# Transposing the next batch's normalised rows on VectorE instead of TensorE

## The reference

```
x = x + LayerNorm(x + relu(x @ W1 + b1) @ W2 + b2) * gamma + beta      # layer 0: x1
x = x + x @ W.T + b                                                    # layer 1: x2
x = x + gated sum of two experts and three shared nets,                # layer 2: x3
        each relu(x @ wi) @ wo with 1024 hidden features
x = x + masked attention pooling of x / count                          # layer 3: out
```

## Time and profile before

| | |
|---|---|
| median of 3 runs | 502.25 us (502.12 to 503.63) |
| the profiled execution's own time | 501.93 us |
| its span in the profile | 500.1 us |
| TensorE busy | 493.7 us, 99% |
| VectorE busy | 349.2 us, 70% |
| ScalarE busy | 260.9 us, 52% |
| GpSimd busy | 235.8 us, 47% |
| TensorE's granted clock | full (2.4 GHz) in all slices |

### The profile page before, as it was taken

How to read it: one execution, slowest core, us unless ns; L and a number is a source line. 1 busy time by engine, 2 the same in 40 slices (tenths; PEclk the granted TensorE clock), 3 DMA queues, 4 the chain that set the end, 5 groups by cost and what they waited for, 6 DMA issues and landing times.

```text
span 500.1 us, 7007 instructions
## 1 busy us (share of the span) xinstructions
PE 493.7 (99%) x2327; PEld 408.6 (82%) x2327; DVE 349.2 (70%) x703; ACT 260.9 (52%) x507; POOL 235.8 (47%) x201
## 2 busy tenths in 40 slices
PE   8999999999999999999999999999999999999996
PEld 5788888888888888888888888888888888888984
DVE  5687226884687799785578689788468779644477
ACT  4655554443457574535346666444345757445234
POOL 1684455445354446444644437444535444745022
PEclk9999999999999999999999999999999999999999
DMA  5865454222265442422227453422222342330002
GB/s 156 185 184 148 111 154 142 86 85 85 86 128 141 116 112 86 127 83 89 80 90 185 105 178 107 127 84 85 85 85 85 102 109 84 102 132 22 0 1 84
DMA packets 77657, 52.97 MB, mean 106 GB/s; under 512 B 40758, under 2 KB 67382, under 8 KB 77622
## 3 DMA queue, kind: packets, MB, share of 16 engines
q1 hardware_dynamic: 75734, 50.44, 35.6%
q10 hardware_dynamic: 1888, 2.10, 1.4%
HBM read 48.33 MB, written 2.10 MB: 101 GB/s over the span
## 4 chain that ended last, share of the span: by engine, by line
PE 98%; DVE 1%; ACT 1%; issue 0%; POOL 0%; DVEq 0%
PE ps_hid L838 14%; PE ps_hid L839 14%; PE ps_hid L843 14%; PE ps_net L900 14%; PE ps_net L895 14%; PE ps_net L896 14%; PE ps_net L867 2%; PE ps_side L537 1%; PE ps_side L541 1%; PE ps_side L536 1%; PE ps_side L547 1%; PE ps_side L550 1%; PE ps_hid L687 1%; PE ps_side L730 1%; PE ps_net L666 1%; PE ps_hid L638 0%
## 5 line engine op out<-in xcount | busy, mean ns | idle before, releaser
L1915 POOL TENSOR_TENSOR wi_lo<-raw_wi,wi_hi 128x512 fp32r<-128x512 f32 x77 | 101.6, 1319 | 207.0 <-ACT wo_hi L1088 109.8
L1109 ACT ACTIVATE hid_hi<-ps_hid 128x512 fp32r<-128x512 f32 x160 | 95.5, 598 | 194.9 <-PE ps_hid L843 193.1
L1823 DVE SCALAR_TENSOR_TENSOR hid_lo<-ps_hid,hid_hi 128x512 fp32r<-128x512 f32 x160 | 109.8, 688 | 114.0 <-ACT hid_hi L1109 112.8
L838 PE MATMUL ps_hid<-x2T_hi,wi_lo 128*128 128x512 f32 (+1 forms) x332 | 125.8, 381 | 0.0
L839 PE MATMUL ps_hid<-x2T_hi,wi_hi 128*128 128x512 f32 (+1 forms) x332 | 125.3, 379 | 0.0
L895 PE MATMUL ps_net<-hid_hi,wo_hi 128*128 128x512 f32 x304 | 118.9, 391 | 0.0
L896 PE MATMUL ps_net<-hid_hi,wo_lo 128*128 128x512 f32 x304 | 118.4, 390 | 0.0
L1916 POOL TENSOR_TENSOR wo_lo<-raw_wo,wo_hi 128x512 fp32r<-128x512 f32 x77 | 104.1, 1352 | 0.0
L843 PE MATMUL ps_hid<-x2T_lo,wi_hi 128*128 128x512 f32 (+1 forms) x332 | 98.9, 379 | 0.0
L900 PE MATMUL ps_net<-hid_lo,wo_hi 128*128 128x512 f32 x304 | 94.0, 390 | 0.0
L839 PEld LDWEIGHTS ps_hid<-x2T_hi,wi_hi 128*128 128x128 f32 x332 | 62.5, 188 | 11.8
(11 more groups left out here) (330 smaller groups left out, 502.7 us busy)
## 6 DMA issues: line engine op xcount, KB each, us to landing
raw_wi<-in_L_cond_share_wi_dram SPq DMA_DIRECT2D x23, 512.0 KB, 3.8
raw_wo<-in_L_cond_share_wo_dram SPq DMA_DIRECT2D x23, 512.0 KB, 4.8
raw_wi<-in_L_cond_expert_wi_dram SPq DMA_DIRECT2D x16, 512.0 KB, 3.8
raw_wo<-in_L_cond_expert_wo_dram SPq DMA_DIRECT2D x16, 512.0 KB, 4.8
next_x2T<-in_x_dram SPq DMA_DIRECT2D x24, 64.0 KB, 4.3
x_rows<-in_x_dram SPq DMA_DIRECT2D x3, 512.0 KB, 4.0
x_rows<-netT SPq DMA_DIRECT2D x48, 32.0 KB, 2.0
out_dram<-out_rows SPq DMA_DIRECT2D x5, 256.0 KB, 5.6
```

The costliest lines, as they stand in the source:

```text
L838: mm(dst, wi_lo[:, w, k, c], x2T_hi[:, k, rows], start=(k == 0), stop=False)
L1109: fn(hid_hi[:, ring(b, q)], ps_hid[:, ring(b, q)], ACT.Relu).then_inc(hid_hi_ready, 1)
L1823: v.scalar_tensor_tensor(out=hid_lo[:, ring(b, q)], in0=ps_hid[:, ring(b, q)], scalar=0.0, in1=f32(hid_hi[:, ring(b, q)]), op0=ALU.max, op ...
L1915: g.tensor_tensor(wi_lo[:, w], raw_wi[:, half % 2, :, c], f32(wi_hi[:, w]), ALU.subtract)
```

## The change

TensorE's transposes of the normalised rows are taken out, with their two semaphore steps. VectorE does them instead. It can transpose 32x32 blocks; to bring block (a, c) of the rows to its place, each instruction takes the 32 partitions of group `a` and writes the 32 partitions of group `c`: 16 instructions for 4 x 4 pairs of groups, each for all 8 (k, r) pairs, 256 elements to a partition. Eight stand in slot 30 and eight in slot 31. They write `next_x2T`, free since slot 21. The scale by gamma and the addition then read this buffer instead of PSUM, both halves in slot 32 behind `xb`, which moves there too. To make room, stage A from `w2` to `norm` runs one slot earlier. `x1_hi`, `x1_lo`, `y` and `base` keep their slots. `adapt` on VectorE gets a wait for its own `subj_w_lo`.

```diff
-    A_SLOT = dict(w1=20, blocks=20, xT=22, w2=25, subj_blocks=25, hid=26, subj_w=27, adapt=28, stats=29, xb=31, norm=30, normT=32, x1_hi=33, x1_lo=35, y=36, base=37)
+    A_SLOT = dict(w1=20, blocks=20, xT=22, w2=24, subj_blocks=24, hid=25, subj_w=26, adapt=27, stats=28, xb=32, norm=29, turn=30, x1=32, x1_hi=33, x1_lo=35, y=36, base=37)
...
+        normT = next_x2T
...
-            def normalised(slot, i):
-                if 0 <= slot - A_SLOT["normT"] < KD:
-                    k = slot - A_SLOT["normT"]
-                    pe.wait_ge(a_dve.sem, a_dve.at(i, "norm"))
-                    for r in range(R):
-                        last = nc.tensor.transpose(ps_side[:, k, r * P:(r + 1) * P], norm[:, r, k * P:(k + 1) * P], ident[:])
-                    last.then_inc(a_pe.sem, 1)
...
+                if slot == A_SLOT["x1"]:
+                    here("turn1")
+                    for k in range(KD):
+                        here(f"xb{k}")
+                        v.scalar_tensor_tensor(out=x1T[:, k], in0=normT[:, k], scalar=gamma[:, k:k + 1], in1=xbT[:, k],
+                                               op0=ALU.mult, op1=ALU.add).then_inc(a_dve.sem, 1)
...
+                if 0 <= slot - A_SLOT["turn"] < 2:
+                    h = slot - A_SLOT["turn"]
+                    here("norm")
+                    for a in (2 * h, 2 * h + 1):
+                        last = turn_rows(a)
+                    last.then_inc(a_dve.sem, 1)
...
+            def turn_rows(a):
+                for c in range(P // BK):
+                    rows = norm[a * BK:(a + 1) * BK].rearrange("p r (k d) -> p k r d", d=P)[:, :, :, c * BK:(c + 1) * BK]
+                    cols = normT[c * BK:(c + 1) * BK].rearrange("p k (r s) -> p k r s", s=P)[:, :, :, a * BK:(a + 1) * BK]
+                    last = v.transpose(cols, rows)
+                return last
```

More of the change, by code:

```diff
@@ L276, in cond_resid_program @@
         evac_dve = Steps(sem("evac_dve"), "g0 g1 g2 g3")
-        a_pe = Steps(sem("a_pe"), "hid adapt0 adapt1 normT0 normT1 y0 y1", 1)
+        a_pe = Steps(sem("a_pe"), "hid adapt0 adapt1 y0 y1", 1)
         a_act = Steps(sem("a_act"), "xhi0 xhi1 hid_below hid_up subj_w_hi x1hi0 x1hi1", 1)
         a_dve = Steps(sem("a_dve"), "w1_hi xT0 xT1 xlo0 xlo1 w2_hi w2_up b2_hi b2_lo subj_wT hid_sum hid_hi hid_lo subj_w_lo sum0 sum1 stats sums mean var_eps "
-                                    "norm xb0 xb1 x1T0 x1T1 x1lo0 x1lo1 x2T0 x2T1", 1)
+                                    "norm turn0 turn1 xb0 xb1 x1T0 x1T1 x1lo0 x1lo1 x2T0 x2T1", 1)
         a_pool = Steps(sem("a_pool"), "w1_lo w2_lo rstd", 1)
@@ L913, in batch @@
                         second_product(b, s, first, last)
-                    if not last:
-                        normalised(q, b + 1)
                     if not first:
@@ L1251, in stage_a @@
                     dve.wait_ge(x_in, 16 * i)
+                    here("subj_w_lo")
                     for t in range(2):
```

## The result

The changed kernel takes **512.81 us** in the median of 5 runs (512.61 to 513.63) against 502.25 before: 1.0207 times as long, with a 95% interval of 1.0196 to 1.0219. Its profiled execution has a span of 510.9 us against 500.1.

What follows compares the result with a forecast made beforehand. TensorE was taken to bound the kernel. Per batch -1.00 (transposes) + 0.65 (adapter) + 3.84 (bank 0) = +3.49, +10.5 us over three batches: 512.7 us from 502.25, forecast range 510.5 to 515, wider range 504.5 to 518.

Steps and rivals of the forecast that it cites:

- What bounds the kernel: TensorE, 98% of the span: 2.72 us per slot without side work; matmuls removed are gained, waits lost, one for one.
- The removed transposes, 1.00 us a batch: Slots 32 to 34 on TensorE: taking the transposes out gains 1.00 us a batch, 3.0 in all, the whole gain.
- The adapter, +0.65 us a batch: Slot 27: TensorE waits 0.76 us instead of 0.11 for `subj_wT_lo`, +0.65 a batch; bounds 0.44 and 1.9.
- The 0.11 us that the wait was said to cost already before: Adapter's second half in the kernel before: its matmul starts about 0.11 us late, waiting for `subj_wT_lo`.
- A transpose at 0.44 us: VectorE's sixteen transposes change output group each time, so do not overlap: 0.44 us each, 7.0 a batch.
- the lower bound of 0.35: VectorE transposes: 0.35 us each if they overlap, 5.6 us a batch; 0.27 was given as the extreme.
- The order in which it goes late: Bank 0 is late next: ScalarE copies it behind `x1_hi` of half 0, and TensorE wants it in slot 34.
- The size of that wait: TensorE's wait on bank 0 in slot 34: 3.84 us a batch, released at 21.97 where 18.13 was due.
- the 3 to 4 named as its sign: Sign of being right: TensorE waits for ScalarE's `netT` three times, 3 to 4 us each.
- the fourth `norm` caught by GpSimd: VectorE's fourth `norm`, issued at 8.86, is held by GpSimd's split at 8.77: VectorE free at 10.2, otherwise 9.2.
- cheaper passage: Rival, chance 0.22: smaller bank wait through slots 29 to 33; 509.7 or 508.4 us, 505.4 with both savings.
- The clock: Within a rival of chance 0.18: TensorE falls to 1.2 GHz after the wait, 2.72 us more a batch, 520.9 us.

Runs made afterwards that it cites:

- e1_no_turn: The kernel before without TensorE's 24 transposes and nothing in their place (that part of the computation left out): 499.46 us, 0.9931 times the kernel before.
- e2_sooner_only: The kernel before with stage A from `w2` to `norm` one slot sooner, transposes still on TensorE: 504.46 us, 1.0038 times the kernel before.
- e6_both_waits: The changed kernel with `x1_hi` one slot later on ScalarE and, in slot 26, `hT_both` and `subj_wT_hi` ahead of the weight split: 500.56 us.
- e7_no_pe_wait: The changed kernel with `x1_hi` one slot later on ScalarE and without TensorE's wait for `subj_wT_lo` before the adapter's second half: 499.25 us.
- e5_same_group: The changed kernel with each of the sixteen transposes writing the partition group it reads (blocks land in wrong groups): 505.64 us.
- e3_copy_first: The changed kernel with `x1_hi` one slot later on ScalarE, so bank 0's copy no longer stands behind it: 501.37 us.
- e4_warm: The changed kernel with ten matmuls of zeros into an unused bank just ahead of TensorE's wait on bank 0: 509.92 us.

## Why the prediction was right, and where it was not

- **What bounds the kernel: right.** TensorE's slots are at 2.72 us wherever nothing makes it wait, before and after, and each term shows one for one in the table.
- **The removed transposes, 1.00 us a batch: right**, by e1_no_turn.
- **The adapter, +0.65 us a batch: right**, +0.65, +0.64 and +0.66, and e2_sooner_only shows it by itself. The mechanism was incomplete: the sum went from ScalarE to GpSimd and never asked when VectorE's queue would be free. That queue ends within 0.1 us of ScalarE's `subj_wT_hi`, so leaving it out changed nothing here, which was luck; e6_both_waits shows that it alone holds most of the wait. The 0.11 us that the wait was said to cost already before is borne out by e7_no_pe_wait, where slot 27 takes 3.71 instead of 3.84.
- **A transpose at 0.44 us: right**, measured 0.45 from start to start (8 in 3.57 and 3.59 us, 422 to 442 ns each), and e5_same_group shows the reason that was given, the change of group. With the group kept it is 0.33, a little under the lower bound of 0.35 that was given for transposes that overlap.
- **The order in which it goes late: right.** ScalarE's copy of bank 0 behind `x1_hi`, in slot 34; e3_copy_first removes nothing but that and all of it is gone.
- **The size of that wait: too large by 1.05 us a batch**, 2.79 instead of 3.84, and by the view of waits 2.5 us, under the 3 to 4 named as its sign. The step that failed is the fourth `norm` caught by GpSimd. `norm` was issued 0.3 us sooner than I had it (102.36, 7.63 into slot 28, where I had 7.93). Three things make that up. I let one small instruction of the statistics through between `wi_lo` and `wo_lo`, and two got through (0.07). The one that is held ends together with `wo_lo`, as the earlier trace rows had shown; my sum ran on as though it began there (0.16). And `wo_lo` ended 0.09 sooner than I had it. The fourth part of `norm` was then ahead of GpSimd's next instruction, which is what had to wait: the four `norm` take 1.38 us together, and `wi_lo` in slot 30 lasts 1.37 instead of 1.29. VectorE came to the next `hid_lo` at 8.93 instead of 10.2; the transposes and the `hid_lo` between them took some 0.3 us more than I had. This is one half of the rival "cheaper passage", which had 0.22, and its 509.7 us is what e4_warm measures (509.92) where the clock does not fall.

```profile
99.03 0.37 DVE L1722 TENSOR_TENSOR mean<-stats 128x4 f32<-128x4 f32 x1
99.32 0.15 DVE L1723 TENSOR_TENSOR mean_gap<-stats 128x4 f32<-128x4 f32 x1
99.39 1.26 DVE L1724 TENSOR_TENSOR var_eps<-stats 128x4 f32<-128x4 f32 x1
```

```profile
99.32 1.31 POOL L1923 TENSOR_TENSOR wo_lo<-raw_wo,wo_hi 128x512 fp32r<-128x512 f32 x1
...
103.51 1.37 POOL L1922 TENSOR_TENSOR wi_lo<-raw_wi,wi_hi 128x512 fp32r<-128x512 f32 x1 [1.19 <-ACT wo_hi L1079]
```

- **The clock: a rival held in part.** I had given the fallen clock a share of 0.18 together with another case, for a pause of 3.8 us and at 2.7 us in each batch, and had put it at nothing in the sum. It fell at a pause of 2.8 us, in two batches of three, and cost 1.6 us each time, 3.2 in all. The two errors, -3 x 1.05 = -3.15 and +3.19, cancel almost exactly. The forecast total was good to 0.1 us by luck; the working was good to about 3 us.
- The Trainium skill ("TensorE: Matmul & The Clock Gate", Part 1) says that an idle TensorE falls to half its clock. The granted clock of 0.50 behind the pauses of the second and third batch, and 1.00 with them filled, agree; the first batch's 1.00 behind the same pause shows that a pause of this length does not always do it.

## What to carry to other kernels

Moving work off a full engine to one that is 70% busy paid here only once its result no longer stood ahead of something else in a third engine's program order: ScalarE's copy of a bank, wanted by TensorE, stood behind an instruction that waited for the moved work. Before such a move, follow each waiting instruction to what is queued behind it, and put what the bound engine needs first. And when a chain is shifted by a slot, look at each wait in it again: one may have a neighbour of another kind, or be no longer needed at all.

## What was not expected of the hardware

- A pause of TensorE of 2.8 us was enough for the granted clock to fall to 1.2 GHz in two of three places (0.50 in the rows of the result), and the same pause did nothing in the third. It costs 1.6 us each time, more than half of the pause again. Ten matmuls of zeros in the pause prevented it in all three places (e4_warm), and a pause 1.5 us shorter did no harm (e5_same_group).
- A VectorE transpose of 256 elements on 32 partitions starts 0.45 us behind the one ahead when each writes another partition group, and 0.33 when both keep to one group.
- Between two GpSimd instructions in a row, two short VectorE instructions that are one behind the other slipped through (99.03 and 99.32 above), and the third waited for the whole of the next one. The other two batches show the same.
